# A decoder layer in one program: another order for the start and the middle of the prologue, and the last feed-forward block in halves

## The reference

```
# 1 linear attention, 32 heads of 8
q, k, v = relu(x @ W_qkv.T); v_pad = [v, 1]
vk = v_pad.T @ k per head; r = (vk @ q); r[:8] / r[8] ; @ W_proj.T + b
# 2 cross attention over ctx, 16 heads of 16
q = rope2d(x @ Wq.T, pos); k = rope2d(ctx @ Wk.T, pos); v = ctx @ Wv.T     # q, k in float16
softmax(q k.T / 4) v @ Wo.T + bo
# 3 feed-forward of low rank
gelu(x @ U1 @ V1 + b1) @ U2 @ V2 + b2        # 256 -> 64 -> 1024 -> 64 -> 256
```

## Time and profile before

| | |
|---|---|
| median of three runs | 529.61 us (529.47 to 529.81) |
| profiled execution | 527.06 us, span 525.3 us, mean granted clock 0.984 |
| busy: PE, PEld | 495.5 us (94%), 335.8 us (64%) |
| busy: DVE, ACT, POOL | 399.2 us (76%), 312.0 us (59%), 345.0 us (66%) |
| first product of block 0 on PE | 12.12 us |
| first shift_t (step 0 begins) | 60.49 us; the next ones 83.54, 107.98, 133.43 us |
| DVE done with block 6 of stage 3 | 513.0 us |
| last product, last y_out | 516.4 us, 522.8 us |

### The profile page before, as it was taken

The page is one execution under the profiler, slowest core; times in us unless marked ns, Lnnn a source line. Parts: engine busy times, 40 slices in busy tenths (PEclk is TensorE's granted clock), DMA queues, the critical chain, the costliest instruction groups (busy, mean ns, idle before and its releaser), DMA issues.

```text
span 525.3 us, 11406 instructions
## 1 busy us (share of the span) xinstructions
PE 495.5 (94%) x4044; PEld 335.8 (64%) x4044; DVE 399.2 (76%) x878; ACT 312.0 (59%) x457; POOL 345.0 (66%) x391
## 2 busy tenths in 40 slices
PE   6997899999999999999999999999979898999992
PEld 3885666777776767676767676767655444545451
DVE  6667877787978887888888888888889983535453
ACT  2653365566656575757574747474737696565650
POOL 6649146868787787777778786868668545433425
PEclk9999799999999999999999999999999999999997
DMA  8574203020402040203020411132000001233232
GB/s 265 130 149 96 65 12 86 12 67 11 106 11 87 11 107 14 84 17 101 17 81 16 104 35 65 37 83 71 9 29 9 29 22 61 80 109 127 105 118 103
DMA packets 29131, 36.01 MB, mean 69 GB/s; under 512 B 5720, under 2 KB 15320, under 8 KB 29080
## 3 DMA queue, kind: packets, MB, share of 16 engines
q1 hardware_dynamic: 28216, 34.37, 22.9%
q10 hardware_dynamic: 864, 0.95, 0.7%
HBM read 23.51 MB, written 8.65 MB: 61 GB/s over the span
## 4 chain that ended last, share of the span: by engine, by line
PE 73%; issue 10%; DVE 7%; POOL 6%; ACT 2%; DMA 1%; POOLq 1%; SPq 0%; ACTq 0%
PE FR L1317 22%; PE BK L1317 12%; PE BK L1505 11%; PE SC L1446 6%; PE SC L1480 6%; PE FR L1406 4%; PE FR L1398 3%; DVE nmax L1090 3%; PE FR L1383 3%; PE FR L1543 2%; POOL rs L666 2%; POOL c_fm L671 2%; PE SC L1317 2%; PE SC L1767 1%; DMA probs<-in_pos 1%
## 5 line engine op out<-in xcount | busy, mean ns | idle before, releaser
L1090 DVE TENSOR_REDUCE nmax<-SC 128x4 f32<-128x1024 f32 x128 | 155.7, 1217 | 23.7 <-PE SC L1446 21.1
L774 ACT ACTIVATE probs<-SC 128x1024 f32<-128x1024 f32 x128 | 130.8, 1027 | 51.2 <-PE SC L1480 51.2
L1505 PE MATMUL BK<-probs,v_aug 128*32 128x256 f32 x1024 | 69.1, 388 | 0.0
L904 ACT ACTIVATE probs<-SC,b_ff 128x512 f32<-128x512 f32 x64 | 38.9, 689 | 24.8 <-PE SC L1772 24.8
L1446 PE MATMUL SC<-k_blk,q_grp 48*128 48x512 f16 x256 | 50.1, 388 | 3.6 <-DVE nmax L1090 2.9
L1480 PE MATMUL SC<-q_grp,k_blk 64*128 64x256 f16 x512 | 49.7, 273 | 3.3 <-ACT probs L774 2.7
L1505 PEld LDWEIGHTS BK<-probs,v_aug 128*32 128x32 f32 x1024 | 26.8, 109 | 26.2 <-issue 11.2
L1480 PEld LDWEIGHTS SC<-q_grp,k_blk 64*128 64x128 f16 x512 | 19.5, 95 | 29.5 <-issue 14.2
L736 ACT ACTIVATE lin_fm_h<-FR 128x512 fp32r<-128x512 f32 x15 | 9.0, 597 | 46.0 <-PE FR L1406 46.0
L666 POOL TENSOR_TENSOR rs<-ve,minus_half 128x2 f32<-128x2 f32 x16 | 11.1, 692 | 35.9 <-DVE nm L1303 35.9
L1783 PE MATMUL FR<-probs,w_u 128*64 128x512 f32 x128 | 30.8, 604 | 0.0
(11 more groups left out here) (260 smaller groups left out, 1534.8 us busy)
## 6 DMA issues: line engine op xcount, KB each, us to landing
x_fm<-in_x_fm SPq DMA_DIRECT2D x16, 256.0 KB, 5.5
x_tm<-in_x_tm SPq DMA_DIRECT2D x16, 256.0 KB, 5.1
x_kept<-x2b SPq DMA_DIRECT2D x16, 256.0 KB, 2.1
x_tm<-x_kept SPq DMA_DIRECT2D x16, 256.0 KB, 2.7
out<-c_fm SPq DMA_DIRECT2D x16, 256.0 KB, 2.0
c_fm<-in_c_fm SPq DMA_DIRECT2D x15, 256.0 KB, 6.0
tables<-rope_tables SPq DMA_DIRECT2D x16, 128.0 KB
k_blk<-k_rope SPq DMA_DIRECT2D x128, 16.0 KB, 1.8
```

The costliest lines, as they stand in the source:

```text
L774: act.activation(probs[:, j % 4], (SC[j % 2] if b == LAST else SB)[:], ACT.Exp, scale=SCALE).then_inc(s_exp, 1)
L904: act.activation(gel[:, f], SC[f % 4 // 2][:].rearrange("p h t -> p (h t)")[:, FB * (f % 2):FB * (f % 2) + FB], ACT.Gelu_apprx_tanh, bias= ...
L1090: dve.tensor_reduce(nmax[:, t, :, 2 * q:2 * q + 2], src[:].rearrange("p (s f) t -> p s f t", s=2), AX.X, ALU.max, negate=True).then_inc(s_ ...
L1505: mm = pe.matmul(BK[q // 2][HP * k:HP * (k + 1), (q % 2) * T:(q % 2 + 1) * T], v_aug[b % NB][:, t, HC * q + k], probs[:, j % 4, k], start= ...
```

## The change

It has three parts.
- **Start.** DVE's low parts of KV1, its second half (C1) and Q1 go between the angle operations, the first one ahead of all three reductions; K2 and V2 stay behind. POOL's split_c(0) waits for Q1's low part instead of C1's. The table of sines is loaded ahead of the first weights, and the sines themselves come behind the two kv1 evictions of item 0. On PE vk(0) goes ahead of k2(0).
- **Middle of the prologue.** k2(2) and v2(2) with their evictions leave step 0 for the prologue; q2(1) moves behind scores1(0,6); x1_t(1), lin(2), lin_t(2) get other places and banks; q's turning for item 1 goes from DVE to POOL, except for `q_halves`, which moves behind the seventh maximum. In step 0 shift_t(0) and its evictions go ahead of scores1(1,0) and row_max(1,0). q1(4) waits for another semaphore.
- **Last block.** It leaves the loops. u2 is made for each half of the tokens in a bank of its own (FR[0], FR[1]), split in halves, multiplied by V2 in halves; DVE takes each half's statistics right behind its addition, and POOL and DVE write one tile of y_out each.

The core of the diff; the waits for banks that only follow from the moves and the definitions of semaphores are left out, and v2(n) in step 0 is treated as k2(n) is:

```diff
 @block.gpsimd
-            pool.wait_ge(s_w_lo, KV1_C1 + 1)
+            pool.wait_ge(s_w_lo, Q1 + 1)
             split_c(0)
...
             weights_lo(DD2, s_ff_lo)
+            rope_q_cos(1)
+            rope_q(1)
             residual_bias(2)
...
-            with pool.Fori(1, NFB) as i:
+            with pool.Fori(1, NFB - 1) as i:
                 norm3(i)
+            last = NFB - 1
+            for h in range(2):
+                pool.wait_ge(s_ve3, 4 * last + 2 * h + 2)
+                pool.tensor_tensor(rs3[:, h], ve3[:, h], minus_half[:], ALU.pow).then_inc(s_rs3, 1)
+                pool.wait_ge(s_rs3, 2 * last + h + 1)
+                pool.wait_ge(s_out[h], 16 * last)
+                pool.tensor_scalar(y_out[:, h, 0], y3[:, h, 0], nm3[:, h, 0:1], rs3[:, h, 0:1],
+                                   ALU.add, ALU.mult).then_inc(s_y, 1)
 @block.scalar
+            act.preload_act_table(ACT.Sin)
             for k in (KV1, KV1_C1, Q1, K2, V2):
                 weights_hi(k)
-            act.wait_ge(s_ang, 8)
-            act.activation(tab[:, 0], red[:, 1], ACT.Sin).then_inc(s_tab, 1)
-            act.activation(tab[:, 1], red[:, 0], ACT.Sin).then_inc(s_tab, 1)
-            act.activation(tab[:, 2], red[:, 0], ACT.Sin, scale=-1.0).then_inc(s_tab, 1)
...
             ev_kv1(0, 1, FR[0])
+            sines()
             ev_q1(0)
...
             norm1(1, 1)
+            ev_k2(2, FR[0])
+            ev_x1(1, FR[1])
             weights_hi(DD2)
-            ev_x1(1, FR[1])
-            ev_q2(1)
-            ev_lint(2, FR[1])
+            ev_v2(2, FR[0])
+            ev_lint(2, BK[1])
+            ev_q2(1, FR[1])
...
-            ev_qf(NFB - 1)
+            for h in range(2):
+                act.wait_ge(s_u2_half, 2 * h + 2)
+                act.activation(qf_fm[0][:, h * T:(h + 1) * T], FR[h][:, 0:T], ACT.Copy).then_inc(s_qf_hi, 1)
 @block.vector
             dve.tensor_scalar(turns[:], turns[:], MAGIC, -MAGIC, ALU.add, ALU.add).then_inc(s_ang, 1)
-            dve.wait_ge(s_ang, 4)
-            dve.scalar_tensor_tensor(red[:], turns[:], -PI_A, ang[:].unsqueeze(1).broadcast_to([P, 2, T]),
-                                     ALU.mult, ALU.add).then_inc(s_ang, 1)
-            dve.wait_ge(s_ang, 5)
-            dve.scalar_tensor_tensor(red[:], turns[:], -PI_B, red[:], ALU.mult, ALU.add).then_inc(s_ang, 1)
             weights_lo(KV1)
+            dve.wait_ge(s_ang, 4)
+            dve.scalar_tensor_tensor(red[:], turns[:], -PI_A, ang[:].unsqueeze(1).broadcast_to([P, 2, T]),
+                                     ALU.mult, ALU.add).then_inc(s_ang, 1)
+            weights_lo(KV1_C1)
+            dve.wait_ge(s_ang, 5)
+            dve.scalar_tensor_tensor(red[:], turns[:], -PI_B, red[:], ALU.mult, ALU.add).then_inc(s_ang, 1)
             dve.wait_ge(s_ang, 6)
             dve.scalar_tensor_tensor(red[:], turns[:], -PI_C, red[:], ALU.mult, ALU.add).then_inc(s_ang, 1)
-            weights_lo(KV1_C1)
+            weights_lo(Q1)
             dve.wait_ge(s_ang, 7)
...
-            for k in (Q1, K2, V2):
-                weights_lo(k)
+            weights_lo(K2)
+            weights_lo(V2)
...
             row_max(0, 3, SB)
+            row_max(0, 4)
             lin(2, (BK[1], BK[0]))
             ev_x1(1, FR[1])
-            row_max(0, 4)
-            rope_q(1)
-            rope_q_sum(1)
             row_max(0, 5, SB)
-            lint(2, FR[1])
+            lint(2, BK[1])
             row_max(0, 6)
+            q_halves(1)
             row_max(0, 7, SB)
             shift(0)
...
+            for h in range(2):
+                half = slice(h * T, (h + 1) * T)
+                dve.wait_ge(s_qf_hi, last + h + 1)
+                dve.tensor_tensor(qf_fm[1][:, half], FR[h][:, 0:T], qf_fm[0][:, half].bitcast(F32), ALU.subtract
+                                  ).then_inc(s_qf_ev, 1)
+            for h in range(2):
+                dve.wait_ge(s_ff_mm, 2 * last + h + 1)
...
+                dve.tensor_tensor(y3[:, h], BK[h][:].rearrange("p (t c) -> p t c", t=TT), x2_blk[:, h], ALU.add
+                                  ).then_inc(s_y3, 1)
+                stats(y3[:, h], (s_y3, 2 * last + h + 1), st3[:, h], s_st3, mv3[:, h], s_mv3, 4 * last + 2 * h)
+                dve.tensor_scalar(ve3[:, h], mv3[:, h, :, 1], LN_EPS, None, ALU.add).then_inc(s_ve3, 1)
+                dve.tensor_scalar(nm3[:, h], mv3[:, h, :, 0], -1.0, None, ALU.mult).then_inc(s_ve3, 1)
+            for h in range(2):
+                dve.wait_ge(s_rs3, 2 * last + h + 1)
+                dve.wait_ge(s_out[h], 16 * last)
+                dve.tensor_scalar(y_out[:, h, 1], y3[:, h, 1], nm3[:, h, 1:2], rs3[:, h, 1:2],
+                                  ALU.add, ALU.mult).then_inc(s_y_dve, 1)
 @block.tensor
             q1(0)
+            vk(0, out=BK[1])
             pe.wait_ge(s_w_lo, K2 + 1)
             k2(0, SA0)
-            vk(0, out=BK[1])
...
             scores1(0, 3)
-            x1_t(1, FR[1])
+            k2(2, FR[0])
+            scores1(0, 4)
             lin(2, 0, BK[1])
             lin(2, 1, BK[0])
-            scores1(0, 4)
-            q2(1)
+            x1_t(1, FR[1])
             scores1(0, 5)
-            lin_t(2, FR[1])
+            v2(2, FR[0])
+            lin_t(2, BK[1])
             scores1(0, 6)
+            q2(1, FR[1])
             scores1(0, 7)
+            pe.wait_ge(s_q2_ev, 2)
             proj1(2)
 def step(b):
+                if b == 0:
+                    shift_t(b)
                 scores1(n1, 0)
...
-                shift_t(b)
+                if b > 0:
+                    shift_t(b)
...
-                if on(n):
+                if on(n) and b > 0:
                     k2(n, FR[1])
...
+            def u2_part(fs, h):
+                for f in fs:
+                    pe.wait_ge(s_gelu, NF * last + f + 5)
+                    mm = pe.matmul(FR[h][R * (f % 2):R * (f % 2) + R, 0:T], w_u2[:, f], gel[:, f, h * T:(h + 1) * T],
+                                   start=(f < 2), stop=(f >= NF - 2))
+                    if f >= NF - 2:
+                        mm.then_inc(s_u2_half, 1)
+            for fs in ((0, 1), (2, 3)):
+                for h in range(2):
+                    u2_part(fs, h)
+            for h in range(2):
+                u2_part(range(4, NF), h)
+            for h in range(2):
+                pe.wait_ge(s_qf_ev, last + h + 1)
+                pe.wait_ge(s_y3, 2 * last + h - 1)
+                for t in range(TT):
...
+                        mm = pe.matmul(BK[h][:, t * C:(t + 1) * C], qf_fm[a_][:, tok], w_d2[b_][:],
+                                       start=(k == 0), stop=(k == 2))
+                mm.then_inc(s_ff_mm, 1)
 @block.sync
+            for h in range(2):
+                sp.wait_ge(s_y, 4 * (NFB - 1) + h + 1)
+                sp.wait_ge(s_y_dve, h + 1)
+                sp.dma_start(a["out"][B - 2 + h], y_out[:, h]).then_inc(s_out[h], 16)
```

More of the change, by code:

```diff
@@ L1306, in _ @@
             raise_p(NFB - 1)
-            with dve.Fori(1, NFB) as i:
+            with dve.Fori(1, NFB - 1) as i:
                 ffn_block(i)
+            last = NFB - 1
+            for h in range(2):
[5 more added lines that the diff above has]
+                dve.wait_ge(s_ff_mm, 2 * last + h + 1)
+                dve.wait_ge(s_x2_in[h], 16 * NFB)
+                dve.wait_ge(s_y, 4 * last - 2 + 2 * h)
+                dve.tensor_tensor(y3[:, h], BK[h][:].rearrange("p (t c) -> p t c", t=TT), x2_blk[:, h], ALU.add
[8 more added lines that the diff above has]
+                                  ALU.add, ALU.mult).then_inc(s_y_dve, 1)
         @block.tensor
@@ L1361, in k2 @@
                 pe.wait_ge(s_cs, n + 1)
-                if on(n + 1) and n >= 2:
+                if n == 2:
+                    pe.wait_ge(s_proj_ev, 2)
+                elif on(n + 1) and n > 2:
                     pe.wait_ge(s_kv1_ev, 2 * (n + 1) + 1)
@@ L1826, in _ @@
             p_ff(LAST)
-            for i in range(2, NFB):
+            for i in range(2, NFB - 1):
                 ffn_block(i)
-            u2_ff4(NFB - 1, 1)
-            v2_ff(NFB - 1)
+            last = NFB - 1
+            def u2_part(fs, h):
[5 more added lines that the diff above has]
+                        mm.then_inc(s_u2_half, 1)
+            pe.wait_ge(s_p_ev, B)
+            h_ff4(last, 0)
+            u2_ff4(last - 1, 1)
+            h_ff4(last, 1)
+            v2_ff(last - 1)
+            pe.wait_ge(s_qf_ev, last)
+            for fs in ((0, 1), (2, 3)):
[7 more added lines that the diff above has]
+                for t in range(TT):
+                    tok = slice((2 * h + t) * P, (2 * h + t + 1) * P)
+                    for k, (a_, b_) in enumerate(((0, 0), (0, 1), (1, 0))):
+                        mm = pe.matmul(BK[h][:, t * C:(t + 1) * C], qf_fm[a_][:, tok], w_d2[b_][:],
+                                       start=(k == 0), stop=(k == 2))
+                mm.then_inc(s_ff_mm, 1)
 def kernel(**inputs):
```

29 lines of the change are left out of this document (20 added, 9 removed).

## The result

| | before | after |
|---|---|---|
| median of four runs each, same chip | 529.54 us (529.35 to 529.81) | 523.26 us (521.59 to 524.67) |
| ratio, with its 95% interval | | 0.988 (0.9845 to 0.9915) |
| profiled execution, span, mean granted clock | 527.06 us, 525.3 us, 0.984 | 521.59 us, 519.8 us, 0.991 |
| PE busy | 495.5 us (94%) | 492.7 us (95%) |

The account below looks back on a forecast made before the run. TensorE, busy 94%, was taken as the bound, so gains come from its waits, half-clock stretches or the ends. Start 1.0, middle 4.4 and tail 2.5 sum to 7.9 us: median 521.7, profiled 519.2; range 519.9 to 524.9.

Parts of the forecast that it names:

- The start: Start of the kernel: reordered low parts, table load and products save 1.0 us, bounds 0.2 to 1.4.
- the meeting with POOL: Middle of the prologue, at 55.1: DVE's clamp of the shift meets POOL's q_sin, costing 0.3 us.
- tables: Start: rope tables come back late; this or a loop's exit takes 1 to 2.5 us off the gain, chance 0.14.
- port: Middle: the shift's second tensor_scalar is held to 56.7, all behind scores2(0,0) 0.6 us later, 522.3; chance 0.12.
- clock: Middle: granted clock falls in the new PE gap between proj1(2) and q1(3), losing 1.2 us, 522.9; chance 0.20.
- The middle up to scores2(0,0): Prologue's middle: scores2(0,0) starts at 58.5 instead of 62.72, 4.2 us less, minus 0.3 for a DVE-POOL meeting.
- k2(2)'s hole: Step 0: taking k2(2) out gives only 0.5 us, because scores1(1,3) behind it needs a maximum.
- v2(2)'s leaving: Step 0: taking v2(2) out gives nothing, since lin_t(3) waits for DVE's lin; PE idles 2 us there.
- The tail: Last block: u2 in two banks, its first half ending early, saves 2.5 us, bounds -0.3 to 2.9.
- The 0.2 for leaving a loop: Tail: allowance of 0.2 us for DVE and POOL running straight code behind a loop's exit.
- The slower case: Steps: the clamp meets q_grp in every step, 1.0 us each, 13 over 13 steps, giving 534.7; chance 0.03.
- the distance of 2.55: Whole kernel: the runs' median of 529.61 us lies 2.55 above the profiled execution's 527.06.

Follow-up runs that it names:

- start_only: The kernel before with only the start's part of the change; 528.22 us, ratio 0.9985.
- tables_early: The changed kernel with b_o2 and x_fm(2) loaded ahead of the rope tables and later loads held until the tables landed; 522.07 us, ratio 0.9874.
- turn_on_dve: The changed kernel with item 1's q_sin and sum moved from POOL to DVE behind the shift, residual_bias(2) waiting for the shift; 523.12 us, ratio 0.9876.
- combined_a: The changed kernel with tables_early and turn_on_dve joined, POOL's residual_bias(2) waiting until the sum is written; 519.89 us, ratio 0.9827.
- after_again: The changed kernel measured once more, unchanged, beside its parts; 522.31 us, ratio 0.9871.
- tail_only: The kernel before with only the last block taken out of the loops and in halves; 526.43 us, ratio 0.9947.

## Why the prediction came out as it did

The median lay inside the range and 1.6 us above the forecast; the profiled execution was at 521.59 for 519.2. The mechanisms of all three parts are there. The start was mis-sized, and so was the meeting with POOL; q_grp came later than reckoned, and one wait (kv1(3) for add1(2)) was not in the sum. The rivals that I had priced singly, tables, port and clock, each came in part.

- **The start, 1.0 forecast, 0.1 measured.** Its reckoning on PE held (kv1 at 10.46 for 10.6, v2(0) at 17.87 for 18.0). What failed is the last step: I wrote that the tables would leave only 0.2 earlier and might be late, and kept the gain of 1.0 all the same, because before's k_cos showed no wait. In `start_only` the read was issued at 21.67 and k_cos released at 29.08, 7.4 us on. Issued at 22.10, as in before, that gives 29.5, and k_cos stood at 29.45: the read had no slack in before either. `start_only` and `tables_early` show it from both sides. It is the rival of the tables, at 0.9 instead of 1 to 2.5.
- **The middle up to scores2(0,0), 4.2 less 0.3 forecast; 3.10 of lead measured, of it 0.14 the start's, so 2.96.** DVE's row without a hole was right to 0.1 us up to the last maximum. Two things failed. One is the meeting with POOL: I had taken it as one operation that meets one, for 0.3. The clamp lost 0.59, and the second tensor_scalar nothing, as I had assumed; but the third operation of the shift, which reads two tiles, met q_grp and lost 0.83. `turn_on_dve` shows the cause. The other is q_grp itself. q2(1)'s eviction ended at 53.51, 53.65 without the start's lead, where I had 53.1, and q_grp at 57.11, so 57.25 for 56.7. scores1(1,0) needs q_grp and began at 57.62, behind shift_t. By this, as an estimate, only 0.4 to 0.5 of the 1.4 us reached scores2(0,0) (59.55, 59.69 without the start, for 58.5), and 0.55 is q_grp's own lateness. The rival of the port had a held second operation and the shift at 56.9: the operation was another, and the shift came at 57.16, 57.30 without the start.
- **k2(2)'s hole, 0.5 forecast, 0.46 measured at its place, and 0.31 lost just ahead of it.** The bound that I took, the maximum before scores1(1,3), is the one that the trace shows (1.10 of wait for nmax). What the sum lacks is kv1(3), which waits for add1(2): DVE reaches that only behind the shift's eviction and row_max(1,0) (58.45), and the shift was late. With the meeting gone, in `combined_a`, kv1(3) starts 0.46 after scores1(1,1) for 0.64, so a part of this wait is the meeting's too. Together the two make 3.24 of lead at lin_t(3) of the 3.10 at scores2(0,0).
- **v2(2)'s leaving, nothing forecast, nothing measured by itself.** Here the sum was right. But I named its hole, "PE idle for 2 us before it", and did not ask what the clock would do there, though the same kind of gap at 55 to 57 was a rival of mine. In the profile of after the clock fell behind the hole, for 1.4. So the rival, with a chance of 0.20 and a price of 1.2, had the mechanism and the size, and the wrong place: the gap at 55 to 57 was passed at 1.00 here, and in `after_again` it was the other way round.
- **The tail, 2.5 forecast, 2.4 measured.** That is by the two traces; the runs of `tail_only` give 2.8, between 1.6 and 4.0. First half-wide product 3.82 us after u2's start for 3.8. The 0.2 for leaving a loop was too much; the last power and y_out took 0.79 and 0.69 for the 0.7 and 0.55 that I had put.
- **The slower case** did not come. The clamp took 0.61 in step 0, for 0.67 in before, 0.18 in each of the next twelve steps, as in before, and 1.10 in step 13, for 1.18.
- **Median against profile.** I took the distance of 2.55 between them as fixed. It was 1.67 after: the profiled execution of before was a good one among its own, further below the median than after's. So of the 2.4 us that the profile lacks of my sum the medians lack 1.6 only. That much of the nearness of 523.26 to the forecast is luck.

What stays open is why the clock falls behind a hole in one execution and not in the next, and how often it falls at each place: no experiment here separated that, and there is one profile of each kernel, two of the changed one.

## What to carry to other kernels

When work moves between DVE and POOL, lay both engines' rows side by side for every operation of the next microseconds, small ones above all: an operation of 0.2 us can take nearly as long as the POOL operation that it meets, and there may be two meetings in a row. When a start is shortened, look for the transfer that was nearly late before, and for what SP has queued behind it. To see what one move is worth, measure between the two instructions on either side of its place: over a longer stretch a late wait or a fall of the clock can hide it. A product taken out of a step "for nothing" may have been what kept PE busy: where it gains no time, leave it in the hole.
